# Layer 0's gated layer: the down projection with the output turned, 512 tokens moving, and the combine weights multiplied into the hidden values

## The chip, the core and the metric

The kernel runs on one core of a Trainium2 chip. The metric is the device time of one execution in microseconds (us), a median of several runs. The engines go by the profile's names: PE is TensorE's matmul and PEld its weight load, DVE is VectorE, ACT is ScalarE, POOL is GpSimd, SP is SyncE, which here only issues DMAs. Every engine works through its own instructions in order and waits on semaphores for the others. PE's clock is granted at one of two levels, 1.2 or 2.4 GHz; the profile writes it as a share of the higher one.

## The reference

Four layers run one after the other on 1,024 tokens (2 batches of 512) of 256 values, each with an attention-like step and a feed-forward step, all with a residual. The change lies in the feed-forward step of layer 0: a gated layer with 8 experts of 1,024 hidden values, all of which see all tokens; every expert's output is scaled by a combine weight of the token.

```python
router_probs = softmax(einsum('bsh,he->bse', x, w_router))
gate_weights = softmax(einsum('bsh,he->bse', x, w_gating) / 0.1)
g = einsum('bsh,ehf->ebsf', x, w_gate)
u = einsum('bsh,ehf->ebsf', x, w_up)
h = silu(g) * u
expert_out = einsum('ebsf,efh->ebsh', h, w_down)
cw = router_probs * gate_weights
cw = cw / (sum(cw, axis=-1, keepdims=True) + 1e-09)
out = einsum('ebsh,bse->bsh', expert_out, cw)
```

`x` here is the layer-normalised input. Since the combine weight of a token and an expert is one number, it may be multiplied into the expert's output or into `h`.

## The kernel before

`gated_layer_phase` (L1039) handles the layer as 32 units of 256 hidden values, four to an expert. Every float32 operand of a matmul is split into a high and a low part, and each product is made of three matmuls (`mm3`, L70: L73 high by high, L74, L75). A unit has four quarters q (L1113): two halves of 128 hidden values by two halves of 512 tokens.

For each unit:

- SP loads the gate and up weights (L1089, 512 KB) and the down weights (L1092, 256 KB), two units ahead at most.
- ACT makes the high parts of the gate and up weights (L1149, a unit ahead), POOL the low parts (L1189); the same for the down weights (L1177, L1202).
- PE computes gate and up of a quarter (L1121 to L1125): 12 matmuls, weights stationary, 512 tokens moving, into one of two gate banks and one of two up banks of PSUM.
- ACT takes silu of the gate (L1157), DVE multiplies it with up (L1217) into `hidden`, which has two slots; ACT rounds that to `h_hi` (L1162) and DVE subtracts to `h_lo` (L1223).
- PE computes the down projection (L1132 to L1139): for 8 chunks of 128 tokens, `h` is stationary and the 256 columns of the down weights move; 6 matmuls to a chunk, 48 to a unit, two chunks to a bank, 12 matmuls after each of which `out_done` counts.
- DVE adds each chunk, times the token's combine weight, to the residual `x` (L1241): 8 instructions to a unit.

The order of the work is written out by hand: `periods` (L1075) gives each engine the periods 0 to 32, the middle 30 of them as a hardware loop of two periods. In period n, PE does gate and up of unit n and then the down projection of unit n - 1, so that the elementwise chain of a unit has the next unit's gate and up (and the one before's down projection) to run beside. Period 32 has only the last down projection. The order on ACT in a period is silu 0, silu 1, high 0, the next unit's gate and up split, silu 2, high 1, silu 3, high 2, high 3, down split.

The router (`l0_router`, L978) runs between periods 0 and 1 (`route(eng)`, L1078): PE makes the logits with 48 matmuls of 16 columns (L1006), DVE and ACT the two softmaxes and the weights `g.cw`, tokens on partitions (L1011 to L1030). Its first user is L1241 in period 1. Ahead of period 0 stands the layer norm (`normaliser`, L159): PE turns the normalised tokens, ACT and DVE write them as `xnT_hi` and `xnT_lo` (L191), in two halves of tokens; PE's first gate matmul needs only the first half (L1116). After the last period DVE also takes the next norm's statistics (L139) of each two chunks as they are done.

Layer 1's expert phase (`l1_experts_phase`, L1426), which the change leaves as it is, already has the form that the change gives to layer 0: its weights are turned on PE (L1377), copied by ACT (L1387), stored by SP to `cw_rows` in DRAM (L1521), loaded back as rows spread over partitions (L1508, two loads of 256 KB for a unit), multiplied in by DVE (L1681), its down projection has stationary weights and 512 tokens moving, adds up in four PSUM banks over all units, and is at the end copied by ACT (L1635), turned back on PE (L1582) and added to `x` by DVE (L1691).

Of the kernel before, what the change touches and what calls it, by code (L numbers as in the profile page):

```python
# [977 lines left out]
def l0_router(nc, ctx, g, d, logits, logits_read):  # L978
# [10 lines left out]
    loaded, split_done = g.sem("r0_loaded"), g.sem("r0_split_done")  # L989
    logits_done, shifted_done, exp_done = g.sem("logits0_done"), g.sem("shifted0_done"), g.sem("exp_r0_done")  # L990
    dve_steps = g.sem("r0_dve_steps")

    def on_sync(sp):
        sp.dma_start(w_raw[:, :, :], d["wr0"]).then_inc(loaded, 16)

    def on_gpsimd(pool):
        split_on_pool(pool, w_raw, w_hi, w_lo, loaded, split_done)

    def on_scalar(act):
        act.wait_ge(shifted_done, 1)  # L1000
        act.activation(exps[:, :, 0, :], shifted[:, :, 0, :], ACT.Exp).then_inc(exp_done, 1)
        act.activation(exps[:, :, 1, :], shifted[:, :, 1, :], ACT.Exp, scale=10.0).then_inc(exp_done, 1)

    def on_tensor(pe):
        pe.wait_ge(split_done, 2)
        router_logits(pe, logits, N, (g.xnT_hi, g.xnT_lo), (w_hi, w_lo)).then_inc(logits_done, 1)  # L1006

    def on_vector(dve):
        own = Chain(dve, dve_steps)
        dve.wait_ge(logits_done, 1)  # L1010
# [4 lines left out]
        dve.sem_inc(shifted_done, 1)  # L1015
        dve.sem_inc(logits_read, 4)
        dve.wait_ge(exp_done, 2)
# [14 lines left out]
        own.wait()  # L1032

    r = Shared()
    r.on_sync, r.on_gpsimd, r.on_scalar, r.on_tensor, r.on_vector = on_sync, on_gpsimd, on_scalar, on_tensor, on_vector
# [3 lines left out]
def gated_layer_phase(nc, g, d, tag, N, weights, make_router):  # L1039
# [6 lines left out]
    with ExitStack() as ctx:  # L1046
# [9 lines left out]
        silu, hidden = sb("silu", [P, 2, 512]), sb("hidden", [P, 2, 512])  # L1056
        gate = ctx.enter_context(nc.psum_tensor(f"gate_{tag}", [P, 2, 512], F32))
        up = ctx.enter_context(nc.psum_tensor(f"up_{tag}", [P, 2, 512], F32))
        out = ctx.enter_context(nc.psum_tensor(f"out_{tag}", [P, TC // 2, 2, D], F32))

        def sem(name):
            return g.sem(f"{name}_{tag}")

        gu_loaded, dn_loaded = [sem("gu_loaded0"), sem("gu_loaded1")], [sem("dn_loaded0"), sem("dn_loaded1")]
        gu_hi_done, gu_lo_done, dn_hi_done, dn_lo_done = sem("gu_hi_done"), sem("gu_lo_done"), sem("dn_hi_done"), sem("dn_lo_done")
        gu_done, silu_done, hidden_done = sem("gu_done"), sem("silu_done"), sem("hidden_done")
        h_hi_done, h_lo_done = sem("h_hi_done"), sem("h_lo_done")
        out_done = sem("out_done")
        out_free = sem("out_free")


        norm = normaliser(nc, ctx, g, tag, out[:, :, :, :].rearrange("p (h k) j e -> p h k (j e)", h=2))
        router = make_router(nc, ctx, g, d, out[:, 0, :, :].rearrange("p j e -> p (j e)")[:, 0:TC * 16].rearrange("p (c n) -> p c n", c=TC), out_free)

        def periods(eng, period, route):  # L1075

            period(0, 0, 1, 1)
            route(eng)  # L1078
            with eng.Fori(0, (N - 2) // 2) as i:
                period(2 * i + 1, 1, i + 1, i + 2)  # L1080
                period(2 * i + 2, 0, i + 2, i + 2)
            period(N - 1, 1, N // 2, None)
            period(N, 0, None, None)

        with nc.Block() as block:
            @block.sync
            def _(sp):
# [3 lines left out]
                def load_dn(n, s):  # L1091
                    sp.dma_start(dn_raw[s][:, :, :], weights[n, :, 2, :, :]).then_inc(dn_loaded[s], 16)  # L1092
# [5 lines left out]
                load_dn(1, 1)  # L1098
                with sp.Fori(0, (N - 2) // 2) as i:
                    for s in range(2):  # L1100
                        sp.wait_ge(gu_lo_done, 2 * i + s + 1)
                        load_gu(2 * i + s + 2, s)
                        sp.wait_ge(dn_lo_done, 2 * i + s + 1)
                        load_dn(2 * i + s + 2, s)

            @block.tensor
            def _(pe):
                def period(n, s, uses, next_uses):
                    first, has_gu = isinstance(n, int) and n == 0, uses is not None
                    if has_gu:  # L1110
                        pe.wait_ge(gu_hi_done, n + 1)
                        pe.wait_ge(gu_lo_done, n + 1)
                        for q in range(Q):  # L1113
# [12 lines left out]
                    if not first:  # L1126
# [3 lines left out]
                        pe.wait_ge(h_hi_done, Q * n)  # L1130
                        pe.wait_ge(h_lo_done, Q * n)
                        for b in range(TC // 2):  # L1132
                            pe.wait_ge(out_free, 4 * (n - 1) + b + 1)
                            for j in range(2):
                                t = slice((2 * b + j) * P, (2 * b + j + 1) * P)
                                for fc in range(FC):
                                    last = mm3(pe, out[:, b, j, :], (h_hi[o][:, fc, t], h_lo[o][:, fc, t]),
                                               (dn_hi[o][:, fc, :], dn_lo[o][:, fc, :]), j == 0 and fc == 0, fc == FC - 1)
                            last.then_inc(out_done, 1)  # L1139

                norm.on_tensor(pe)
                pe.sem_inc(out_done, 4)
                periods(pe, period, router.on_tensor)

            @block.scalar
            def _(act):
                def split_gu(n, s, uses):
# [3 lines left out]
                def period(n, s, uses, next_uses):  # L1151
# [7 lines left out]
                    def high(q):  # L1159
                        fc, half = divmod(q, 2)  # L1160
                        act.wait_ge(hidden_done, Q * n + q + 1)
                        act.activation(h_hi[s][:, fc, half * 512:(half + 1) * 512], hidden[:, q % 2, :], ACT.Copy).then_inc(h_hi_done, 1)  # L1162
# [3 lines left out]
                    if not (isinstance(n, int) and n == 0):  # L1166
                        act.wait_ge(out_done, 4 * n)
# [8 lines left out]
                    act.wait_ge(dn_loaded[s], 16 * uses)  # L1176
                    act.activation(dn_hi[s][:, :, :], dn_raw[s][:, :, :], ACT.Copy).then_inc(dn_hi_done, 1)  # L1177
# [5 lines left out]
                periods(act, period, router.on_scalar)  # L1183

# [23 lines left out]
            def _(dve):  # L1208
                def period(n, s, uses, next_uses):
                    first = isinstance(n, int) and n == 0  # L1210

                    def product(q):
                        dve.wait_ge(silu_done, Q * n + q + 1)
                        if not (first and q < 2):
                            dve.wait_ge(h_hi_done, Q * n + q - 1)
                            dve.wait_ge(h_lo_done, Q * n + q - 1)
                        dve.tensor_tensor(hidden[:, q % 2, :], silu[:, q % 2, :], up[:, q % 2, :], ALU.mult).then_inc(hidden_done, 1)  # L1217

                    def low(q):
                        fc, half = divmod(q, 2)  # L1220
                        t = slice(half * 512, (half + 1) * 512)
                        dve.wait_ge(h_hi_done, Q * n + q + 1)
                        dve.tensor_tensor(h_lo[s][:, fc, t], hidden[:, q % 2, :], f32(h_hi[s][:, fc, t]), ALU.subtract).then_inc(h_lo_done, 1)  # L1223

                    if uses is not None:
                        product(0)
                        product(1)
                        low(0)
                        product(2)
                        low(1)  # L1230
                        product(3)
                        low(2)
                        low(3)
                    if not first:
                        dve.wait_ge(out_free, 4 * n)
                        for b in range(TC // 2):
                            dve.wait_ge(out_done, 4 * n + b + 1)
                            for j in range(2):
                                c = 2 * b + j
                                weight = g.cw[:, c, bass.ds(n - 1, 1)]  # L1240
                                last = dve.scalar_tensor_tensor(g.x[:, c, :], out[:, b, j, :], weight, g.x[:, c, :], ALU.mult, ALU.add)  # L1241
                            last.then_inc(out_free, 1)
                            if uses is None:
                                dve.wait_ge(out_free, 4 * n + b + 1)
# [1775 lines left out]
```

## Time and profile before

| what | us |
|---|---|
| runs: 1546.78, 1550.95, 1555.5; median | 1550.95 |
| the profiled execution, its own time | 1558.52 |
| span of its instructions | 1556.7 |
| granted clock of PE, mean over the span | 0.943 of 2.4 GHz |
| PE busy | 1410.2 (91%) |
| DVE busy | 899.8 (58%) |
| ACT busy | 695.5 (45%) |
| POOL busy | 332.9 (21%) |
| DMA, bytes moved | 110.83 MB, 71 GB/s |

Busy time counts an engine's computing instructions only. Matmuls overlap: a row of 400 ns for one matmul does not mean that the next one starts 400 ns later, so the pace of PE is read from the starts, not from the lengths. A stretch view gives, for a stretch of the span, the busy time and number of instructions of each engine and the mean granted clock. A timeline row gives the start from the beginning of the span, the length, engine, line, output and inputs, and in brackets the idle time before it and who ended it. A line of a helper (L73 to L75, L191, L206, L139) stands for all who call it; the tile's name tells them apart.

### The profile page before, as it was taken

To read this page: it belongs to the slowest core of one execution; us is meant where nothing else is said; L and a number is where in the kernel's file an instruction comes from. 1 tells how busy PE (TensorE), PEld (TensorE's weight loads), DVE (VectorE), ACT (ScalarE), POOL (GpSimd) and SP (SyncE) were. 2 spreads that over 40 slices of the span, in tenths; PEclk is the share of its full clock that TensorE was granted. 3 is DMA by queue.
4 is the path that set the end of the run, shared out by engine and by line. 5 is a ranking of instruction groups with operands and counts; after the bars stand their busy time and mean duration, and the time that the engine had idled before them with its cause. 6 is when DMAs were issued, how large, how long until landed. Compare 5 with 4: busy or idle time off the path is not lost. (4 is left out here: it accounts for less than half of the span.)

```text
span 1556.7 us, 24649 instructions
## 1 busy us (share of the span) xinstructions
PE 1410.2 (91%) x8362; PEld 1131.1 (73%) x8362; DVE 899.8 (58%) x1719; ACT 695.5 (45%) x1134; POOL 332.9 (21%) x348
## 2 busy tenths in 40 slices
PE   5799999799999999999998799999899786876994
PEld 4544444588888888888887777888678675765883
DVE  6778887655555555555556544444466455535556
ACT  5266667244344344344343265555443324443432
POOL 2101224212222222222221123333300033231100
PEclk8889999899999999999999799999999789897997
DMA  6811311111111111111100124555232115223000
GB/s 227 243 30 35 76 39 25 60 42 40 61 40 40 60 41 40 61 40 40 61 27 14 49 75 122 141 142 141 86 98 68 50 56 178 83 83 105 1 1 27
DMA packets 63703, 110.83 MB, mean 71 GB/s; under 512 B 10235, under 2 KB 39421, under 8 KB 62749
## 3 DMA queue, kind: packets, MB, share of 16 engines
q1 hardware_dynamic: 61773, 104.93, 23.1%
q0 software_dynamic: 1872, 5.13, 0.9%
q8 instruction: 36, 0.59, 0.2%
q14 instruction: 22, 0.18, 0.0%
HBM read 90.91 MB, written 18.97 MB: 71 GB/s over the span
## 5 line engine op out<-in xcount | busy, mean ns | idle before, releaser
L1217 DVE TENSOR_TENSOR hidden_l<-silu_l,up_l 128x512 f32<-128x512 f32 x128 | 88.1, 688 | 220.2 <-ACT silu_l L1157 220.2
L1157 ACT ACTIVATE silu_l<-gate_l 128x512 f32<-128x512 f32 x128 | 76.6, 599 | 308.6 <-PE up_l L75 308.6
L851 DVE TENSOR_REDUCE maxima<-a_scores 128x1 f32<-128x512 f32 x256 | 164.7, 685 | 41.0 <-PE a_scores L790 39.7
L73 PE MATMUL out_l<-dn_hi_l,h_hi_l 128*128 128x256 f32 x560 | 159.5, 285 | 5.4 <-DVE h_lo_l L2328 5.4
L818 ACT ACTIVATE probs<-b_scores 128x1024 f32<-128x1024 f32 x128 | 131.1, 1024 | 66.5 <-PE b_scores L747 64.5
L74 PE MATMUL out_l<-dn_lo_l,h_hi_l 128*128 128x256 f32 x560 | 159.1, 284 | 0.0
L75 PE MATMUL out_l<-dn_hi_l,h_lo_l 128*128 128x256 f32 x560 | 159.1, 284 | 0.0
L1189 POOL TENSOR_TENSOR gu_lo_l<-gu_raw_l,gu_hi_l 128x1024 fp32r<-128x1024 f32 x31 | 74.4, 2399 | 299.0 <-ACT gu_hi_l L1149 299.0
L73 PE MATMUL gate_l<-xnT_hi_n,gu_hi_l 128*128 128x512 f32 x280 | 112.6, 402 | 15.0 <-issue 11.8
L1241 DVE SCALAR_TENSOR_TENSOR x_sb<-out_l,cw,x_sb 128x256 f32<-128x256 f32 x256 | 109.0, 478 | 22.4 <-PE out_l L75 18.1
L73 PEld LDWEIGHTS out_l<-dn_hi_l,h_hi_l 128*128 128x128 f32 x560 | 108.4, 194 | 8.5 <-issue 5.9
L74 PE MATMUL gate_l<-xnT_lo_n,gu_hi_l 128*128 128x512 f32 x280 | 111.9, 400 | 0.0
L73 PE MATMUL up_l<-xnT_hi_n,gu_hi_l 128*128 128x512 f32 x280 | 111.7, 399 | 0.0
L75 PE MATMUL gate_l<-xnT_hi_n,gu_lo_l 128*128 128x512 f32 x280 | 111.5, 398 | 0.0
L74 PE MATMUL up_l<-xnT_lo_n,gu_hi_l 128*128 128x512 f32 x280 | 111.4, 398 | 0.0
L75 PE MATMUL up_l<-xnT_hi_n,gu_lo_l 128*128 128x512 f32 x280 | 111.2, 397 | 0.0
L74 PEld LDWEIGHTS out_l<-dn_lo_l,h_hi_l 128*128 128x128 f32 x560 | 108.2, 193 | 1.7
L75 PEld LDWEIGHTS out_l<-dn_hi_l,h_lo_l 128*128 128x128 f32 x560 | 108.0, 193 | 0.0
L1223 DVE TENSOR_TENSOR h_lo_l<-hidden_l,h_hi_l 128x512 fp32r<-128x512 f32 x128 | 102.3, 800 | 3.2
L1681 DVE TENSOR_TENSOR hidden_l<-silu_l,spread_l 128x512 f32<-128x512 f32 x64 | 44.3, 693 | 91.6 <-ACT silu_l L1608 91.6
L1608 ACT ACTIVATE silu_l<-front_l,b_l 128x512 f32<-128x512 f32 x80 | 55.0, 688 | 89.4 <-PE front_l L75 89.4
L790 PE MATMUL a_scores<-k_stack,q_stack 96*128 96x512 bf16 x256 | 85.1, 405 | 8.4 <-DMA q_stack<-q_stacks 5.4
(474 smaller groups left out, 3422.5 us busy)
## 6 DMA issues: line engine op xcount, KB each, us to landing
gu_raw_l<-w_units SPq DMA_DIRECT2D x32, 512.0 KB, 3.6
spread_l<-cw_rows SPq DMA_DIRECT2D x64, 256.0 KB, 3.9
dn_raw_l<-w_units SPq DMA_DIRECT2D x32, 256.0 KB, 2.7
k_stack<-k_stacks SPq DMA_DIRECT2D x8, 768.0 KB, 5.8
staged_l<-w_experts SPq DMA_DIRECT2D x24, 256.0 KB, 3.4
up_raw_l<-w SPq DMA_DIRECT2D x40, 128.5 KB, 3.5
dn_raw_l<-w SPq DMA_DIRECT2D x40, 128.0 KB, 2.1
phi_a<-fside SPq DMA_DIRECT2D x8, 512.0 KB, 3.3
```

The costliest lines, as they stand in the source:

```text
L73: pe.matmul(out, lhs[0], rhs[0], start=start, stop=False, skip_group_check=True)
L74: pe.matmul(out, lhs[0], rhs[1], start=False, stop=False, skip_group_check=True)
L75: return pe.matmul(out, lhs[1], rhs[0], start=False, stop=stop, skip_group_check=True)
L790: pe.matmul(a_scores[:, k % 2, :], q_stack[buf][0:MAXROW, h, at:at + P], k_stack[buf][0:MAXROW, h, kh * 512:(kh + 1) * 512], start=True, s ...
L818: act.activation(probs[u % 4][:, :, :], b_scores[:, u % 2, :, :], ACT.Exp, scale=SCALE).then_inc(exp_done, 1)
L851: dve.tensor_reduce(maxima[k // 16][:, i // 2, i % 2:i % 2 + 1], a_scores[:, k % 2, :], X, ALU.max).then_inc(a_read, 1)
L1157: act.activation(silu[:, q % 2, :], gate[:, q % 2, :], ACT.Silu).then_inc(silu_done, 1)
L1189: pool.tensor_tensor(gu_lo[s][:, :, :, :], gu_raw[s][:, :, :, :], f32(gu_hi[s][:, :, :, :]), ALU.subtract).then_inc(gu_lo_done, 1)
L1217: dve.tensor_tensor(hidden[:, q % 2, :], silu[:, q % 2, :], up[:, q % 2, :], ALU.mult).then_inc(hidden_done, 1)
L1223: dve.tensor_tensor(h_lo[s][:, fc, t], hidden[:, q % 2, :], f32(h_hi[s][:, fc, t]), ALU.subtract).then_inc(h_lo_done, 1)
L1241: last = dve.scalar_tensor_tensor(g.x[:, c, :], out[:, b, j, :], weight, g.x[:, c, :], ALU.mult, ALU.add)
L1608: act.activation(silu[:, q, :], up[:, q, :], ACT.Silu, bias=b1[s][:, :]).then_inc(silu_done, 1)
```

## The change

- **Down projection.** The down weights are stationary (128 hidden by 128 output values), 512 tokens of `h` move. A unit has 24 matmuls of 512 columns in place of 48 of 256. The sums stay in four PSUM banks (two halves of tokens by two halves of the outputs, turned) over all 32 units; only the first unit's down projection starts the banks.
- **Combine weights.** DVE multiplies `hidden` by `spread`, the unit's weights as a row on all 128 partitions, before `h_hi` and `h_lo` are made. `hidden` has four slots now. L1241 goes.
- **Router.** It runs ahead of period 0, on all engines, with its logits in the second gate bank, so PE waits for both halves of the norm first. After quarter 1 of unit 0, PE turns the weights into output banks (8 transposes), ACT copies them (after the split of unit 1's gate and up weights), SP stores them to DRAM, waits, and then loads the rows of units 0 and 1, spread. In the loop, SP loads unit n + 2's row once unit n's scaled values are done. Row and down weights share a semaphore.
- **Period 0.** ACT and DVE have another order in it: first all four silus and products, then the four scaled values, the four high and four low parts.
- **End.** ACT copies the four banks to `outT`, PE turns them back (16 transposes), and DVE adds them to `x` in four instructions with the statistics between them.
- Periods 1 and 2 are written out ahead of the loop (now 14 rounds of two periods).

The diff, cut to its core:

```diff
         def periods(eng, period, route):
+            route(eng)
             period(0, 0, 1, 1)
-            route(eng)
-            with eng.Fori(0, (N - 2) // 2) as i:
-                period(2 * i + 1, 1, i + 1, i + 2)
-                period(2 * i + 2, 0, i + 2, i + 2)
+            period(1, 1, 1, 2)
+            period(2, 0, 2, 2)
+            with eng.Fori(0, (N - 4) // 2) as i:
+                period(2 * i + 3, 1, i + 2, i + 3)
+                period(2 * i + 4, 0, i + 3, i + 3)
...
+                router.store_weights(sp)
+                load_spread(0, 0)
+                load_spread(1, 1)
                 with sp.Fori(0, (N - 2) // 2) as i:
                     for s in range(2):
                         sp.wait_ge(gu_lo_done, 2 * i + s + 1)
                         load_gu(2 * i + s + 2, s)
                         sp.wait_ge(dn_lo_done, 2 * i + s + 1)
                         load_dn(2 * i + s + 2, s)
+                        sp.wait_ge(hidden_done, Q * (2 * i + s + 1))
+                        load_spread(2 * i + s + 2, s)
...
                                 pe.wait_ge(silu_done, Q * n + q - 1)
-                                pe.wait_ge(hidden_done, Q * n + q - 1)
+                                pe.wait_ge(product_added, Q * n + q - 1)
+                            if first and q == 1:
+                                pe.wait_ge(router.shifted_done, 1)
+                            if first and q == 2:
+                                router.turn_weights(pe)
...
-                        for b in range(TC // 2):
-                            pe.wait_ge(out_free, 4 * (n - 1) + b + 1)
-                            for j in range(2):
-                                t = slice((2 * b + j) * P, (2 * b + j + 1) * P)
+                        for h in range(2):
+                            t = slice(h * 512, (h + 1) * 512)
+                            for dc in range(KC):
+                                e = slice(dc * P, (dc + 1) * P)
                                 for fc in range(FC):
-                                    last = mm3(pe, out[:, b, j, :], (h_hi[o][:, fc, t], h_lo[o][:, fc, t]),
-                                               (dn_hi[o][:, fc, :], dn_lo[o][:, fc, :]), j == 0 and fc == 0, fc == FC - 1)
+                                    last = mm3(pe, out[:, h, dc, :], (dn_hi[o][:, fc, e], dn_lo[o][:, fc, e]),
+                                               (h_hi[o][:, fc, t], h_lo[o][:, fc, t]), isinstance(n, int) and n == 1 and fc == 0, not has_gu and fc == FC - 1)
...
                     silu_of(0)
                     silu_of(1)
-                    if not (isinstance(n, int) and n == 0):
-                        act.wait_ge(out_done, 4 * n)
+                    if isinstance(n, int) and n == 0:
+                        split_gu(1, 1, 1)
+                        router.copy_weights(act)
+                        silu_of(2)
+                        silu_of(3)
+                        for q in range(Q):
+                            high(q)
+                        split_dn(s, uses)
+                        return
+                    act.wait_ge(down_returned, n)
                     high(0)
...
+                    def scale(q):
+                        half = q % 2
+                        if q == 0:
+                            dve.wait_ge(dn_spread_loaded[s], 32 * uses)
+                        dve.wait_ge(product_added, Q * n + q + 1)
+                        dve.tensor_tensor(hidden[:, q, :], hidden[:, q, :], spread[s][:, half * 512:(half + 1) * 512], ALU.mult).then_inc(hidden_done, 1)
...
+                    if first:
+                        for q in range(Q):
+                            product(q)
+                        for q in range(Q):
+                            scale(q)
+                        for q in range(Q):
+                            low(q)
+                        return
+                    dve.wait_ge(h_lo_done, Q * n)
+                    product(0)
+                    scale(0)
+                    product(1)
+                    scale(1)
+                    low(0)
...
+                for m in range(TC // 2):
+                    dve.wait_ge(down_returned, N + 2 * KC + m + 1)
+                    dve.tensor_tensor(g.x[:, 2 * m:2 * m + 2, :], g.x[:, 2 * m:2 * m + 2, :],
+                                      back[m].rearrange("p (j e) -> p j e", j=2), ALU.add).then_inc(product_added, 1)
+                    dve.wait_ge(product_added, Q * N + m + 1)
+                    take_stats(dve, g, (2 * m, 2 * m + 1))
```

## Rows read from the trace of the kernel before

**Rows 1.** Stretch view, 14 units: length, each engine's busy us, clock, DMA share, GB/s.

```profile
586.21:819.45 233.24, 233.24 (x1345) 206.73 (x1344) 126.34 (x224) 93.81 (x147) 51.77 (x28) 1.00 0.14 45
```

**Rows 2.** Groups by line of 28 units (busy us, mean ns | idle before, releaser).

```profile
L1241 DVE SCALAR_TENSOR_TENSOR x_sb<-out_l,cw,x_sb 128x256 f32<-128x256 f32 x224 | 95.4, 478 | 19.7 <-PE out_l L75 15.8
L1223 DVE TENSOR_TENSOR h_lo_l<-hidden_l,h_hi_l 128x512 fp32r<-128x512 f32 x112 | 89.6, 800 | 2.8
L1217 DVE TENSOR_TENSOR hidden_l<-silu_l,up_l 128x512 f32<-128x512 f32 x112 | 77.1, 688 | 191.3 <-ACT silu_l L1157 191.3
L1157 ACT ACTIVATE silu_l<-gate_l 128x512 f32<-128x512 f32 x112 | 67.1, 599 | 272.1 <-PE up_l L75 272.1
L1149 ACT ACTIVATE gu_hi_l<-gu_raw_l 128x1024 fp32r<-128x1024 f32 x28 | 29.5, 1054 | 0.0
```

**Rows 3.** Time order on PE, one unit: first matmul of down, gate/up, down (start, length).

```profile
586.21 0.28 PE L73 MATMUL out_l<-dn_hi_l,h_hi_l 128*128 128x256 f32 x1
591.97 0.40 PE L73 MATMUL gate_l<-xnT_hi_n,gu_hi_l 128*128 128x512 f32 x1
602.87 0.28 PE L73 MATMUL out_l<-dn_hi_l,h_hi_l 128*128 128x256 f32 x1
```

**Rows 4.** Time order on PE, layer 1's experts: a down projection's first matmul, and the next.

```profile
1004.58 0.40 PE L73 MATMUL out_l<-h_hi_l,dn_hi_l 128*128 128x512 f32 x1
1007.35 0.40 PE L73 MATMUL front_l<-xnT_hi_n,up_hi_l 128*128 128x512 f32 x1
```

**Rows 5.** Time order at the layer's front: normaliser, router logits, router, first down projection.

```profile
302.77 2.47 DVE L191 TENSOR_TENSOR xnT_lo_n<-out_l,xnT_hi_n 128x512 fp32r<-128x512 f32 x4
...
321.90 0.36 PE L75 MATMUL out_l<-wr_hi_r,xnT_lo_n 128*128 128x16 f32 x1
322.54 0.36 PE L75 MATMUL out_l<-wr_hi_r,xnT_lo_n 128*128 128x16 f32 x1
322.94 0.29 DVE L1011 TENSOR_REDUCE top<-out_l 128x16 f32<-128x128 f32 x1 [3.19 <-PE out_l L75]
326.23 0.68 DVE L1030 TENSOR_TENSOR cw<-both,total 128x64 f32<-128x64 f32 x4
...
336.31 0.28 PE L73 MATMUL out_l<-dn_hi_l,h_hi_l 128*128 128x256 f32 x1
```

**Rows 6.** The stretch view: first gate matmuls; after the logits; PE idle since 294.65.

```profile
305.30:307.70 2.40, 2.40 (x7) 1.86 (x6) 0.00 (x0) 0.31 (x1) 0.00 (x0) 0.50 0.26 106
...
322.70:328.00 5.30, 5.30 (x13) 4.16 (x14) 3.14 (x15) 1.68 (x3) 0.00 (x0) 0.50 0.35 137
...
297.00:298.00 1.00, 0.00 (x0) 0.00 (x0) 0.64 (x8) 0.90 (x1) 0.00 (x0) 0.76 0.00 0
```

**Rows 7.** Time order in layer 1: its weights turned, copied, stored, spread.

```profile
919.54 1.03 PE L1377 MATMUL front_l<-ident_sb,exps 128*64 128x128 f32 x8
...
920.61 1.02 ACT L1387 ACTIVATE cwT<-front_l 64x1024 f32<-64x1024 f32 x1 [1.61 <-PE front_l L1377]
...
921.66 0.55 SPq L1521 DMA_DIRECT2D cw_rows<-cwT  x1
924.66 1.17 SPq L1508 DMA_DIRECT2D spread_l<-cw_rows  x2
```

**Rows 8.** DMA issues (KB, median us to landing); landing of layer 1's 64 spread loads.

```profile
gu_raw_l<-w_units SPq DMA_DIRECT2D x32, 512.0 KB, 3.6
...
DMA to landing us min/median/max: 3.4/3.9/4.9
```

**Rows 9.** Time order at the end: gated layer's last matmul and statistics; layer 1's.

```profile
847.50 0.28 PE L75 MATMUL out_l<-dn_hi_l,h_lo_l 128*128 128x256 f32 x1
...
849.18 0.75 DVE L139 BATCH_NORM_STATS2 stats_sb<-x_sb 128x6 f32<-128x256 f32 x2
...
1116.66 0.39 PE L75 MATMUL out_l<-h_hi_l,dn_lo_l 128*128 128x512 f32 x1
...
1122.37 0.75 DVE L139 BATCH_NORM_STATS2 stats_sb<-x_sb 128x6 f32<-128x256 f32 x2
```

More of the change, by code:

```diff
@@ L975, in router_logits, with l0_router @@
     return last
-def l0_router(nc, ctx, g, d, logits, logits_read):
+def l0_router(nc, ctx, g, d, logits, banks):
     def sb(name, shape, dt=F32):
@@ L1066, in gated_layer_phase @@
         gu_done, silu_done, hidden_done = sem("gu_done"), sem("silu_done"), sem("hidden_done")
[L1067 to L1073, printed above, removed]
+        h_outT_done, h_lo_done = sem("h_hi_or_outT_done"), sem("h_lo_done")
@@ new lines, in period, with with_halves, return_output @@
+                        if has_gu:
+                            last.then_inc(down_returned, 1)
+                def with_halves(pe):
+                    norm.wait_half(pe, 0)
+                    norm.wait_half(pe, 1)
+                    router.on_tensor(pe)
+                def return_output(pe):
+                    for h in range(2):
+                        pe.wait_ge(h_outT_done, Q * N + KC * (h + 1))
+                        for c in range(4):
+                            for dc in range(KC):
+                                last = pe.transpose(back[2 * h + c // 2][:, c % 2 * D + dc * P:c % 2 * D + (dc + 1) * P],
+                                                    outT[:, h, dc, c * P:(c + 1) * P], g.ident[:, :])
+                            if c % 2 == 1:
+                                last.then_inc(down_returned, 1)
@@ L1147, in split_gu, with copy_output @@
+                def copy_output(act):
+                    for h in range(2):
+                        for dc in range(KC):
+                            act.wait_ge(down_returned, N + KC * h + dc + 1)
+                            act.activation(outT[:, h, dc, :], out[:, h, dc, :], ACT.Copy).then_inc(h_outT_done, 1)
                 def split_gu(n, s, uses):
@@ L1175, in period @@
                     high(3)
[L1176 to L1177 removed]
+                    split_dn(s, uses)
                 norm.root(act)
@@ L1221, in low @@
                         t = slice(half * 512, (half + 1) * 512)
[L1222 to L1244, printed above, removed]
-                                take_stats(dve, g, (2 * b, 2 * b + 1))
+                        dve.wait_ge(h_outT_done, Q * n + q + 1)
+                        dve.tensor_tensor(h_lo[s][:, fc, t], hidden[:, q, :], f32(h_hi[s][:, fc, t]), ALU.subtract).then_inc(h_lo_done, 1)
+                    if uses is None:
+                        return
[6 more added lines that the diff above has]
+                            low(q)
+                        return
+                    dve.wait_ge(h_lo_done, Q * n)
[4 more added lines that the diff above has]
+                    low(0)
+                    product(2)
+                    scale(2)
+                    low(1)
+                    product(3)
+                    scale(3)
+                    low(2)
+                    low(3)
                 norm.moments(dve)
```

79 lines of the change are left out of this document (54 added, 25 removed).

## The prediction

> **What bounds the kernel now.** The page shows PE busy for 91% of the span, but busy time hides the pace of matmuls, so I read the layer that changes stage by stage. The stretch view of 14 of its units [rows 1] has PE busy for all of 233.24 us at the full clock: 16.66 us a unit. DVE is busy 126 us of it, ACT 94, POOL 52, the DMA engines 0.14. No PE wait is left in the steady part, so only PE work taken out shortens it. The time order on PE [rows 3] splits a unit: 48 matmuls of the down projection, 256 columns each, from 586.21 to 591.97, 5.76 us or 0.120 each; 48 of gate and up, 512 columns each, to 602.87, 10.90 us or 0.227 each. The columns are the same (48 x 256 = 24 x 512), but two narrow matmuls take 0.240 and a wide one 0.227. That difference is what the change can win; what it moves to the front and the end of the layer is what it pays.
>
> **Steady part: minus 9.9 us.** A unit's down projection becomes 24 wide matmuls. At the pace of gate and up, which have the same form and stand between the same engines' work, they take 24 x 0.227 = 5.45 us, 0.31 less [rows 3]. Layer 1's down projection is nearer in operands (stationary down weights, banks kept over units) and slower: 12 in 2.77 us, 0.231 each [rows 4], so 5.54 us and 0.22 less. I take the first, since the surroundings are this layer's own, and keep the second as the end: 32 units give 9.9, at worst 7.0 us. No row shows wide matmuls faster than 0.227 over a unit, so I allow no more gain.
>
> The Trainium skill speaks against this: "TensorE: Matmul & The Clock Gate", section "Wait — 56ns, not 53.3ns?", states a fixed cost of about 2.5 ns for each warm matmul above its columns. By it, an estimate, 24 matmuls fewer would give 0.06 us a unit and 1.9 us in all. The trace disagrees: 0.120 us is 13 ns above 256 columns at 2.4 GHz, and 0.227 is 14 above 512 [rows 3].
>
> DVE loses 8 instructions of L1241 at 478 ns, 3.8 us a unit, and gains 4 multiplications, 2.8 us at the 688 ns of L1217 [rows 2]. Both lie beside PE and are worth nothing. The new chain of a unit (product, scale, high, low) is one multiplication a quarter longer. After the last quarter's silu come product and scale 3 at 0.69 each, low 2 and low 3 at 0.80 and ACT's work between them, some 4 us in all; PE needs them only after a down projection (5.45) and the next gate and up (10.9). Only the last unit has just the 5.45 us as cover, and there POOL's down split comes after it with about half a us to spare by my count. SP's new loads, 512 KB a unit, bring the DMA share of 0.14 [rows 1] to less than 0.3. SP waits for the scaled values before a row is loaded, and the next gate load is queued behind that; it is needed a period and a half later. The loop written out further changes no work.
>
> **Front: plus 11.7 us.** Before, the first down projection starts at 336.31 [rows 5]. I build its start after the change.
> - PE waits for both halves of the norm, which DVE ends at 302.77 + 2.47 = 305.2 [rows 5]. The clock then is at 0.50, the 1.2 GHz level [rows 6], after an idle PE. The 48 logit matmuls run there: three take from 321.90 to 322.54 at that level, 0.213 each [rows 5], so 10.2 us, to 315.6. That the clock is still low behind the logits, I take from the place behind them before the change, where it stood at 0.50 for 5.3 us with 13 gate matmuls [rows 6].
> - So the first 13 gate and up matmuls of unit 0 take 5.3 us again, the other 35 take 35 x 0.227 = 7.9, the 8 transposes 1.0 [rows 7]: unit 0 ends at 329.8. Unit 1's first two quarters, 5.45 us, end at 335.3.
> - Beside this runs the way of the weights. DVE's router needs 326.23 + 0.68 - 322.94 = 4.0 us from the logits [rows 5] and is done at 320, ahead of PE, so it costs nothing. PE turns the weights after quarter 1, at 315.6 + 5.3 + 11 x 0.227 = 323.4. ACT then has silu 1 (to 324.2), the split of L1149 (1.05, to 325.3; [rows 2]) and the copy (1.02, to 326.3; [rows 7]). From store to spread load layer 1 takes 924.66 - 921.66 = 3.0 [rows 7]: 329.4. The 512 KB row lands after 3.6 us by the gate load of the same size, 3.9 by the median of layer 1's half as large rows, 4.9 by their slowest [rows 8]; two of those one after the other, 9.8, are my far end. I take 4.2, a little above both medians: 333.6.
> - Only then can DVE scale: 4 x 0.69, 4 low parts at 0.80, and the product 0 of unit 1 at 0.69 [rows 2], 6.65 us, all in DVE's order, to 340.2. ACT's high parts, its down split and silu 0 of unit 1 are queued in the same way and end earlier. PE's quarter 2 of unit 1 needs the bank that this product frees. So **PE stands from 335.3 to 340.2**, 4.9 us; SP's gate load for unit 2 waits behind the store too, but has until about 342.
> - After a PE idle since 294.65 the clock's mean was already 0.76 in the stretch 297 to 298 [rows 6], so I expect it to fall in this gap as well. What it costs is 5.3 us for 13 matmuls that take 2.95 at full pace, 2.35. The two remaining quarters then take 5.45 + 2.35, and the first down projection starts at 348.0, **11.7 us later**. If the clock holds, 9.4.
>
> **End: plus 4.0 us.** Before, DVE follows the last down projection bank by bank, and the statistics end 849.18 + 0.75 - 847.50 = 2.4 us after PE's last matmul starts. Layer 1's end has the new form, copies, transposes, then four additions with statistics that DVE does one after the other: 1122.37 + 0.75 - 1116.66 = 6.5 us [rows 9]. The row is the same form and the same shapes, so I give it no more than half a us either way.
>
> **Sum.** 11.7 + 4.0 - 9.9 = +5.8 us. The profiled execution's own time of 1558.52 would become 1564.3. It is 7.6 us above the median of the runs shown; the terms are differences, so they hold for either, and on the median of 1550.95 the sum gives **1556.8 us**, 0.4% slower. A difference of 0.5%, 7.75 us, is about what a measurement of this kernel can tell from none, so my forecast is no change that can be told, on the slow side.
>
> **The rivals.**
> - *The row of weights lands late, and the kernel is slower.* Place: unit 0's scale on DVE, with PE standing in unit 1. Each us of landing after 4.2 is a us of the end, since nothing behind it has slack. For it: no row shows a spread load of 512 KB, and unit 1's row and unit 2's gate weights are issued right behind it. Against it: 512 KB of gate weights land in 3.6 [rows 8]. It decides from a landing of 4.2 + 1.95 = 6.15 us on, where the sum passes 7.75; at the far end of 9.8 it is +11.4, 1562.4 us. Chance 0.2.
> - *PE does not stand.* If the weights come as early as PE can use them, unit 1 ends at 329.8 + 10.9 = 340.7, the front costs 4.4, and the sum is 4.4 + 4.0 - 9.9 = -1.5: 1549.5 us. For it: ACT, DVE and SP may overlap more closely than row by row. Against it: the chain from 323.4 to 340.2 is in order throughout, with 4.9 us to make up. Chance 0.17.
> - *Wide matmuls gain less.* If a wide down matmul starts every 0.231 us as in layer 1 [rows 4], the gain is 7.0 and the sum +8.7, 1559.7 us. Chance 0.08. By the 2.5 ns of the Trainium skill's "TensorE: Matmul & The Clock Gate" (above), as an estimate, it would be 11.7 + 4.0 - 1.9 = +13.8, 1564.8 us.
> - *A real gain* needs front and end together below 2 us; I find no row for it, since the additions at the end alone cost 4.0.
>
> **How the numbers follow.** The forecast has 0.55. Its own range goes from 9.4 + 3.5 - 9.9 = +3.0 (the clock holds) to some +8. The range over all cases reaches down past the case without the stall, 1549.5, by the 2.5 us that a median of runs between 1546.78 and 1555.5 may well move, and up to the late row with the slower pace, 11.4 + 2.9 = +14.3: **1547 to 1565 us**. For the same reason I count part of each case on either side of the bound. Faster by over 0.5%: 0.06 (most from the case without the stall). Slower by over 0.5%: 0.17 of the forecast, 0.16 of the late row and 0.05 of the slower pace, 0.38. Within 0.5%: the rest, 0.56.
>
> **What would show it.** In the profile after the change: 24 wide down matmuls to a unit in about 5.45 us and a unit in 16.35, with PE never idle between; logits from about 305 to 316 at a granted clock of 0.5; a single PE gap of about 5 us before quarter 2 of unit 1, ended by DVE's product behind the spread load, and 1.2 GHz after it; the first down projection 12 us later than before; statistics 6.5 us after the last down matmul. The forecast is wrong if the unit does not get shorter, if PE waits in the steady part for the scaled values or the row, or if there is no gap in unit 1.

## The result and the profile after

The changed kernel takes 1557.93 us (median of 20 runs, 1550.62 to 1563.69), the kernel before 1553.17 (20 runs beside them, 1546.78 to 1557.01). The medians lie 4.8 us apart; over the runs the kernel takes 1.0034 times as long, 95% interval 1.0020 to 1.0048, which is 3.1 to 7.5 us more. The forecast was 5.8 us more, within half a per cent. It came out, but not by its own sum: two terms, the front and the steady part, were off in the same direction, by 3.4 us together, and part of the loss lies where the prediction did not look. That the total fits is in part luck.

One profiled execution gives the parts. The first rows are the stretch view of the kernel after (length; busy us of PE, PEld, DVE, ACT, POOL; clock; DMA share; GB/s): 14 units of the steady part, then the logits, the first gate matmuls, and the stretch behind PE's stand.

```profile
589.86:818.34 228.48, 228.48 (x1009) 189.19 (x1008) 121.94 (x169) 84.76 (x140) 56.70 (x28) 1.00 0.23 78
...
305.28:315.30 10.02, 10.02 (x48) 10.02 (x48) 0.00 (x0) 0.00 (x0) 0.00 (x0) 0.50 0.00 0
315.51:320.78 5.27, 5.27 (x14) 4.11 (x14) 3.14 (x15) 1.69 (x3) 0.00 (x0) 0.50 0.00 0
...
337.99:341.40 3.41, 3.41 (x8) 2.73 (x9) 2.69 (x4) 1.58 (x2) 1.04 (x2) 0.52 0.44 165
```

A unit takes 228.48 / 14 = 16.32 us instead of 16.66 [rows 1], with PE busy throughout. The logits run at 0.50, 10 us long, and the gate matmuls behind them at 0.50 for 5.27 (5.30 before [rows 6]).

The time order of the kernel after shows one unit (first matmuls of down, gate, next down), then the layer's front and its end (start, length, what ended the wait before it).

```profile
589.86 0.39 PE L73 MATMUL out_l<-h_hi_l,dn_hi_l 128*128 128x512 f32 x1
...
595.30 0.39 PE L73 MATMUL gate_l<-xnT_hi_n,gu_hi_l 128*128 128x512 f32 x1
...
606.18 0.39 PE L73 MATMUL out_l<-h_hi_l,dn_hi_l 128*128 128x512 f32 x1
...
305.28 0.35 PE L73 MATMUL gate_l<-wr_hi_r,xnT_hi_n 128*128 128x16 f32 x1 [2.70 <-DVE xnT_lo_n L191]
...
323.54 1.03 PE L1039 MATMUL out_l<-ident_sb,cw 128*32 128x128 f32 x8
...
326.20 0.34 SPq L1048 DMA_DIRECT2D cw_rows<-cw0T  x1
328.20 0.33 SPq L1124 DMA_DIRECT2D spread_l<-cw_rows  x1
332.21 2.50 DVE L1297 TENSOR_TENSOR hidden_l<-hidden_l,spread_l 128x512 f32<-128x512 f32 x4 [0.80 <-DMA spread_l<-cw_rows]
334.63 2.49 DVE L1303 TENSOR_TENSOR h_lo_l<-hidden_l,h_hi_l 128x512 fp32r<-128x512 f32 x4
337.15 0.69 DVE L1290 TENSOR_TENSOR hidden_l<-silu_l,up_l 128x512 f32<-128x512 f32 x1
337.99 0.77 PE L73 MATMUL gate_l<-xnT_hi_n,gu_hi_l 128*128 128x512 f32 x1 [2.49 <-DVE hidden_l L1290]
...
345.06 0.39 PE L73 MATMUL out_l<-h_hi_l,dn_hi_l 128*128 128x512 f32 x1
...
845.32 0.40 PE L75 MATMUL out_l<-h_hi_l,dn_lo_l 128*128 128x512 f32 x1
...
846.19 0.69 DVE L1340 TENSOR_TENSOR x_sb<-x_sb,gate_l 128x512 f32<-128x512 f32 x1 [7.89 <-PE gate_l L1193]
...
851.04 0.75 DVE L139 BATCH_NORM_STATS2 stats_sb<-x_sb 128x6 f32<-128x256 f32 x2
```

Down takes 5.44 us where [rows 3] had 5.76. In the front, read the releasers: DVE was idle for only 0.80 us until the row of weights landed, then worked in order for 5.6 us, and PE stood 2.49 us for the product at its end. The first down projection starts at 345.06 against 336.31 [rows 5], and the statistics end 6.47 us behind the start of the last down matmul, against 2.4 [rows 9].

All kernels of this study were read in these parts. Front: from the layer's first aggregate on DVE (296.53 after, 297.14 before) to the first down matmul. Middle: to the start of the last one. End: to the end of the last statistics. Layer 1: from its own first aggregate to that of the next phase. Single runs of one kernel differ by up to 13 us, and the longer ones were granted the lower mean clock (kernel after: 1550.62 us at 0.943, 1563.69 at 0.932); the parts of layer 0 and layer 1 repeat within 0.15 us (last two rows of the table against the first two). Each ratio is to runs of the kernel before that were made beside that kernel (medians of 1551.91 to 1553.80 us).

| kernel | front | middle | end | layer 0 | layer 1 | median us (runs) | ratio to before, 95% |
|---|---|---|---|---|---|---|---|
| before | 39.17 | 511.19 | 2.43 | 552.79 | 252.88 | 1553.17 (20) | |
| after | 48.53 | 500.26 | 6.47 | 555.26 | 254.07 | 1557.93 (20) | 1.0034 (1.0020 to 1.0048) |
| e1_narrow | 48.27 | 511.19 | 6.36 | 565.82 | 249.20 | 1567.86 (6) | 1.0095 (1.0072 to 1.0118) |
| e2_row_ready | 46.08 | 500.25 | 6.47 | 552.80 | 250.83 | 1555.84 (1) | |
| e3_order | 46.20 | 500.36 | 6.46 | 553.02 | 250.72 | 1553.30 (12) | 1.0000 (0.9984 to 1.0016) |
| e4_before_router_first | 43.38 | 511.19 | 2.42 | 556.99 | 250.74 | 1554.71 (1) | |
| e5_front | 37.21 | 504.04 | 6.47 | 547.72 | 251.05 | 1549.84 (12) | 0.9970 (0.9956 to 0.9983) |
| e6_end | 48.43 | 501.16 | 4.62 | 554.21 | 252.18 | 1554.98 (1) | |
| e7_both | 37.22 | 504.91 | 4.63 | 546.76 | 251.00 | 1549.55 (12) | 0.9975 (0.9960 to 0.9991) |
| e8_early_gate | 37.18 | 501.28 | 4.63 | 543.09 | 254.10 | 1544.65 (6) | 0.9948 (0.9934 to 0.9962) |
| e9_after_again | 48.45 | 500.25 | 6.47 | 555.17 | 254.06 | 1558.88 (1) | |
| e10_before_again | 39.18 | 511.19 | 2.42 | 552.79 | 252.89 | 1554.88 (1) | |

### The profile page after: what moved, and what is told of

The parts are those of the page before. It is cut to its first block and busy times, and to the rows that moved or that the text cites. A ratio compares the mean times of both kernels' runs of the same rounds, so it can differ in the third digit from the quotient of the medians.

```text
span 1556.3 us, 22704 instructions
## 1 busy us (share of the span) xinstructions
PE 1407.6 (90%) x7618; PEld 1099.0 (71%) x7618; DVE 888.1 (57%) x1595; ACT 679.4 (44%) x1124; POOL 343.8 (22%) x348
## 5 line engine op out<-in xcount | busy, mean ns | idle before, releaser
L73 PE MATMUL out_l<-h_hi_l,dn_hi_l 128*128 128x512 f32 x416 | 162.2, 390 | 0.8 <-POOL dn_lo_l L1749 0.8
L75 PE MATMUL out_l<-h_hi_l,dn_lo_l 128*128 128x512 f32 x416 | 162.6, 391 | 0.0
L74 PE MATMUL out_l<-h_lo_l,dn_hi_l 128*128 128x512 f32 x416 | 162.5, 391 | 0.0
L1265 POOL TENSOR_TENSOR gu_lo_l<-gu_raw_l,gu_hi_l 128x1024 fp32r<-128x1024 f32 x31 | 84.8, 2735 | 270.2 <-ACT gu_hi_l L1217 270.2
L1297 DVE TENSOR_TENSOR hidden_l<-hidden_l,spread_l 128x512 f32<-128x512 f32 x128 | 108.4, 849 | 7.2 <-DMA spread_l<-cw_rows 0.8
L1230 ACT ACTIVATE h_hi_l<-hidden_l 128x512 fp32r<-128x512 f32 x128 | 80.0, 626 | 34.1 <-DVE hidden_l L1297 34.1
L73 PEld LDWEIGHTS out_l<-h_hi_l,dn_hi_l 128*128 128x128 f32 x416 | 78.3, 188 | 18.4 <-issue 1.2
L74 PEld LDWEIGHTS out_l<-h_lo_l,dn_hi_l 128*128 128x128 f32 x416 | 78.2, 188 | 17.1
L75 PEld LDWEIGHTS out_l<-h_hi_l,dn_lo_l 128*128 128x128 f32 x416 | 78.1, 188 | 16.6
```

The source lines that it names most:

```text
L73: pe.matmul(out, lhs[0], rhs[0], start=start, stop=False, skip_group_check=True)
L74: pe.matmul(out, lhs[0], rhs[1], start=False, stop=False, skip_group_check=True)
L75: return pe.matmul(out, lhs[1], rhs[0], start=False, stop=stop, skip_group_check=True)
L1265: pool.tensor_tensor(gu_lo[s][:, :, :, :], gu_raw[s][:, :, :, :], f32(gu_hi[s][:, :, :, :]), ALU.subtract).then_inc(gu_lo_done, 1)
L1297: dve.tensor_tensor(hidden[:, q, :], hidden[:, q, :], spread[s][:, half * 512:(half + 1) * 512], ALU.mult).then_inc(hidden_done, 1)
```

## The experiments

**e1_narrow: what makes the unit shorter.** In the down projection:

```
+ for part in range(2):                      # 256 tokens each
+     t = slice(h * 512 + part * 256, ...)
-     mm3(pe, out[:, h, dc, :], (dn...), (h_hi[o][:, fc, t], ...))
+     mm3(pe, out[:, h, dc, a], (dn...), (h_hi[o][:, fc, t], ...))
```

> The kernel after with one thing undone: the down projection moves 256 tokens in one matmul, 48 matmuls of 256 columns to a unit instead of 24 of 512; operands, banks, order and everything else stay. Theory (a matmul costs some 14 ns above its columns here, so two narrow ones take 0.240 us and a wide one 0.227): first to last down matmul goes from 500.3 us to the 511.2 us of the kernel before, 0.34 us a unit; the layer and the time grow by 10.9 us, to about 1569. Rival (the fixed cost of a matmul is 2.5 ns, as the Trainium skill's page TensorE: Matmul & The Clock Gate states, and the unit became shorter for another reason, the orientation or DVE's additions): 500.3 plus 1.9, 502.2 us, and about 1560.

Measured: the middle is 511.19 us, that of the kernel before to the hundredth, and 10.93 more than in the kernel after. Orientation, banks kept over the units and the work taken from DVE do nothing for it; the number of matmuls does everything. The theory holds, and the rival's 502.2 is excluded. Every matmul here has a weight load of its own, so no run parts the cost of a matmul from that of its weight load.

**e2_row_ready: is it the way through DRAM that makes PE stand?**

```
+ spread[s] <- weights[s, 0:1, 0:2]   (s = 0, 1, ahead of store_weights)
  router.store_weights(sp)
- load_spread(0, 0); load_spread(1, 1)
```

> The kernel after, but the rows of weights of units 0 and 1 are filled from the gate weights in DRAM, right behind the first loads, so that no row waits for router, turn, copy and store (units 0 and 1 are therefore scaled by other numbers; the store still runs, behind the two loads). Theory A, the prediction's (the way of the weights through DRAM makes PE stand in unit 1): the gap of 2.5 us and the low clock behind it go, and the first down projection starts 3.9 us earlier, 44.6 us after the layer's first aggregate instead of 48.5. Theory B (DVE was idle for only 0.8 us before the first scale; its order, four scales and four low parts ahead of unit 1's product 0, makes PE stand): the gap shrinks by 0.8, to 1.7 us, still ended by product 0, and the first down projection comes about 1 us earlier.

Measured, from the time order and the stretch view of e2_row_ready:

```profile
337.54 0.69 DVE L1291 TENSOR_TENSOR hidden_l<-silu_l,up_l 128x512 f32<-128x512 f32 x1
338.37 0.47 PE L73 MATMUL gate_l<-xnT_hi_n,gu_hi_l 128*128 128x512 f32 x1 [1.60 <-DVE hidden_l L1291]
```

```profile
338.37:341.77 3.40, 3.40 (x15) 2.85 (x16) 2.70 (x4) 1.98 (x3) 1.03 (x2) 1.00 0.54 181
```

PE still stands, for 1.60 instead of 2.49 us: theory B. But the clock stays at 1.00 behind the shorter stand, and so the front shrinks by 2.45 us and not by 1: 0.9 of standing and the 1.6 that the low clock had cost.

**e3_order: DVE's order.** Two more buffers of hidden; DVE and ACT of unit 0:

```
  for q in range(Q): product(q)
+ product(0, 1); product(1, 1)        # unit 1's
  for q in range(Q): scale(q)
```

> The kernel after with another order in the first two units: DVE makes unit 1's products 0 and 1 (in two further buffers of hidden) ahead of unit 0's scales, and ACT makes the two silus ahead of unit 0's high parts; the way of the weights is as it was. Theory B (DVE's order sets the gap): no gap in unit 1, the clock stays up, unit 1 ends 2.5 + 1.4 us earlier and the first down projection starts 44.6 us after the layer's first aggregate (48.5 before this edit); the time falls by 3.9, to about 1554. Theory A (the landing sets it): PE stands in front of the first down projection instead, for as long as it stood before, and the first down stays near 48. Rival C (the stall is only moved on): the first down is earlier, but unit 1's own scales are now late, a gap of 1 to 2 us appears before the second down projection, and the layer gains less than 2 us.

None of the three. The stand in unit 1 is gone, as B says; the front gains 2.3 us and not 3.9, since PE now stands in front of the first down projection, but not for the row, as A had it. Time order of e3_order:

```profile
339.67 0.62 ACT L1207 ACTIVATE dn_hi_l<-dn_raw_l 128x512 fp32r<-128x512 f32 x1
340.44 2.19 POOL L1281 TENSOR_TENSOR dn_lo_l<-dn_raw_l,dn_hi_l 128x512 fp32r<-128x512 f32 x1 [12.47 <-ACT dn_hi_l L1207]
...
342.73 0.47 PE L73 MATMUL out_l<-h_hi_l,dn_hi_l 128*128 128x512 f32 x1 [1.96 <-POOL dn_lo_l L1281]
```

The down weights had long been loaded, but ACT splits them behind four high parts, and GpSimd's low part follows. That queue had been hidden under the stand. GpSimd's low part also took 2.19 us here, beside DVE's low parts, and 1.30 with DVE idle beside it (kernel after, 348.64); the last section says more of this pair. The middle stays at 500.36, so rival C, a stand that is only moved on, is out too. The runs fall by more than layer 0's 2.24 us, because layer 1 is 3.35 shorter as well (below).

**e4_before_router_first: the move alone.**

```
- period(0, 0, 1, 1); route(eng)
+ route(eng); period(0, 0, 1, 1)      # PE: both halves of the norm first
```

> The kernel before with the router alone moved ahead of unit 0, behind both halves of the norm, as in the kernel after; additions on DVE, narrow down projection and everything else as before. Theory (the logits at the low clock cost 10.2 us where they took 5.9 behind unit 0; the start 1.1 us later because both halves are waited for; only one low stretch with gate matmuls instead of one and a half, minus 1.7): the first down projection starts 3.7 us later than in the kernel before, 42.9 us after the layer's first aggregate instead of 39.2. Rival (48 logit matmuls cost the same wherever they stand): at most 1.5 us later, 40.7.

Measured: 4.21 us (43.38 against 39.17), half a us above the theory's 3.7 and far from the rival's 1.5. Its stretches are those of the kernel after: logits 10.24 us and the gate matmuls behind them 5.26, all at 0.50. The move of the router is thus nearly half of the front's 9.36; the turn (0.8), the stand (2.49) and the low clock behind it (1.6) make 4.9 of the other 5.15.

**e5_front: another order of the front.** On e3_order:

```
+ unit 0 on PE: q0, logits of chunks 0-3, q1, logits 4-7, q2, q3
+ unit 1: turn_weights, q0 ... q3; down(0): wait for h=0, then for h=1
+ ACT: split_dn(0) ahead of the high parts; split_gu(2) between them
+ DVE, unit 0: scales and low parts of h=0, then of h=1; router between products 1 and 2
- route(eng)
```

> The kernel after with the front put in another order (steady part and end as they are): gate and up of unit 0 start behind the first half of the norm; the logits stand in a bank of the down sums, 24 of them behind quarter 0 and 24 behind quarter 1; the weights are turned ahead of unit 1; unit 1's products 0 and 1 come ahead of unit 0's scales in two further buffers; the first down projection waits for each half of the tokens by itself. Theory (the front of the kernel after costs 9.4 us because logits and 13 gate matmuls run at the low clock, PE starts 1.1 us later, and PE stands for 2.5 us): 24 logits between wide matmuls leave the clock up, the low clock is paid once (some 8 gate matmuls), PE does not stand, and the first down projection starts 39 to 41 us after the layer's first aggregate (48.5 in the kernel after, 39.2 in the kernel before); the time falls by 8, to about 1550, 3 us under the kernel before. Rival A (logits bring the clock down wherever they stand): 42 to 44 us. Rival B (the row of weights lands too late for the earlier down projection): PE stands in front of the first down by 3 us or more, 42 to 44 us, at full clock until then.

Measured: the front is 37.21 us, 2 under the kernel before; ratio 0.997. Neither rival A nor B, and better than the theory, since here the first quarter of unit 0 ran at 1.00 as well (0.50 in the kernel before [rows 6]). Stretch view of e5_front, the first quarter, both groups of logits and the gate matmuls behind the second:

```profile
304.72:307.53 2.81, 2.81 (x12) 2.33 (x13) 1.05 (x2) 0.84 (x1) 0.00 (x0) 1.00 0.00 0
307.53:310.13 2.60, 2.60 (x26) 2.59 (x24) 0.69 (x1) 0.60 (x1) 0.00 (x0) 1.00 0.00 0
312.96:315.56 2.60, 2.60 (x26) 2.60 (x24) 0.69 (x1) 2.38 (x3) 0.42 (x1) 1.00 0.00 0
315.56:319.99 4.43, 4.43 (x15) 3.47 (x15) 3.14 (x15) 2.13 (x4) 1.95 (x1) 0.61 0.03 6
```

24 logits between wide matmuls run at full clock in 2.60 us, and the clock falls only behind the second group. The first quarter takes 2.81 us; in the time order of the kernel before it takes 4.49, from the first gate matmul of this quarter to that of the next:

```profile
304.19 0.77 PE L73 MATMUL gate_l<-xnT_hi_n,gu_hi_l 128*128 128x512 f32 x1 [1.01 <-DVE xnT_lo_n L191]
...
308.68 0.39 PE L73 MATMUL gate_l<-xnT_hi_n,gu_hi_l 128*128 128x512 f32 x1
```

That is 1.7 of the 2.0 us. It was not forecast: PE stands for 4.86 us ahead of the normaliser's transposes in both kernels, and why the clock was up again sooner in e5_front is not shown. Without it the front would take 38.9 us, about the lower end of the theory's 39 to 41. The middle lost 3.8 us again, by a stand inside the first down projection. Time order of e5_front:

```profile
334.41 3.49 DVE L1315 TENSOR_TENSOR hidden_l<-hidden_l,spread_l 128x512 f32<-128x512 f32 x2
334.59 2.76 POOL L1279 TENSOR_TENSOR gu_lo_l<-gu_raw_l,gu_hi_l 128x1024 fp32r<-128x1024 f32 x1 [1.26 <-ACT gu_hi_l L1217]
...
339.44 0.47 PE L73 MATMUL out_l<-h_hi_l,dn_hi_l 128*128 128x512 f32 x1 [1.80 <-DVE h_lo_l L1321]
```

Two scales take 3.49 us and end at 337.90, half a us after GpSimd's low part (337.35).

**e6_end: the end overlapped.** In the last period:

```
+ if (h, dc) == (1, KC - 1): return_output(pe, 0)   # ahead of the last bank
```

> The kernel after with the end overlapped: the sums of the first 512 tokens are turned back between the last two banks of the down projection instead of behind all of them, so that DVE's first two additions with their statistics run beside PE's last bank. Theory (the 6.5 us behind the last down matmul are DVE's four additions with statistics, 5.6 us, behind a copy and transposes): the last statistics end about 1.1 us earlier, 554.2 us for the layer instead of 555.3. Rival (copy and transposes of the second half set the end): less than 0.4 us.

Measured: layer 0 is 1.05 us shorter, 554.21, as the theory says. PE's last down matmul starts 0.9 later, behind the transposes, and DVE ends 1.05 earlier: DVE's four additions set the end, but for 0.32 us for which DVE now waits for the second half's transposes.

**e7_both** is e5_front with e6_end.

> The edits of e5_front and e6_end together, output complete. Theory: the two add, since one lies ahead of the first and the other behind the last down projection: 9 us less than the kernel after, about 1549, ratio to the kernel before 0.997. Rival (one of the two is given back in the other's place): no more than the better of the two alone.

Measured: layer 0 shrinks by 8.50 us; 7.54 and 1.05 alone. They add in the profile. The runs can't tell e7_both from e5_front: its ratio is 0.9975 (0.9960 to 0.9991), and the gain of 1 us is below what they resolve. They also show less than the profile does: to the end of layer 1 the profile is 7.95 us ahead of the kernel before, the runs 3.9 (1.4 to 6.2).

**e8_early_gate: GpSimd out of DVE's way.** On e7_both:

```
+ load_gu(2, 0)                  # SP, ahead of store_weights
+ split_gu(2, 0, 2)              # ACT, behind copy_weights
+ split_gu(2, 0)                 # GpSimd, in period 0
```

> e7_both with one more edit: unit 2's gate weights are loaded ahead of the store of the router's weights, and ACT and GpSimd split them before the row of weights lands instead of between unit 0's second scales. Theory (in e5_front DVE's second pair of scales, 334.41 to 337.90, took 3.49 us where two take 1.38, because GpSimd's low part of the gate weights ran from 334.59 to 337.35 and a DVE multiplication with both operands in SBUF cannot run beside it): the two scales take 1.4 us, PE no longer stands in front of the second half of the first down projection (1.8 us) and the clock does not fall behind it; first to last down shrinks by 3.8 us, from 504.9 to 501.1, and the time to about 1546, 0.995 of the kernel before. Rival (DVE waited for ACT or for the row, not for GpSimd): the scales stay at 3.5 us and nothing is gained.

Measured, time order of e8_early_gate:

```profile
334.03 1.28 DVE L1325 TENSOR_TENSOR hidden_l<-hidden_l,spread_l 128x512 f32<-128x512 f32 x2
```

The two scales take 1.28 us, the stand is gone, and the middle is 501.28 us (3.6 less). The theory holds, the rival is out. 1544.65 us, ratio 0.9948: the fastest kernel of the study, under the kernels before and after. The gain lies in layer 0, 9.70 us shorter than before; layer 1 is 1.2 us longer. The profiled execution, 1549.52 us, is the slowest of its six.

**e9_after_again, e10_before_again: where the rest of the loss lies.** No edit.

> The kernel after, unchanged, once more. Its profile showed layer 0 longer by 2.5 us, the runs the whole by 4.8; its layer 1 took 254.1 us against 252.9, with the clock at 0.50 for 10 us from the layer's aggregate where the kernel before had 5. Theory (the clock in layer 1's front differs from execution to execution): layer 0 again takes 555.3 us within 0.3, layer 1 another time than 254.1, by 1 us or more. Rival (layer 1 is longer because of the change): 254.1 within 0.5, and the clock again at 0.50 for 10 us.

> The kernel before, unchanged, once more, for the same question. Theory (from execution to execution): layer 0 again takes 552.8 us within 0.3, layer 1 another time than 252.9 by 1 us or more. Rival (a property of the kernel): 252.9 within 0.5.

The rival holds, both times: layer 1 takes 254.06 and 252.89 us, as in the first profiles. It belongs to the kernel. In the stretch from 5 to 10 us behind layer 1's first aggregate, first the kernel after:

```profile
878.83:883.83 5.00, 4.46 (x13) 3.22 (x12) 2.15 (x4) 3.43 (x6) 0.55 (x1) 0.50 0.38 143
```

and the kernel before:

```profile
877.03:882.03 5.00, 3.95 (x20) 2.99 (x19) 2.85 (x5) 3.68 (x7) 0.55 (x2) 0.92 0.34 127
```

PE's work is the same there; it runs at 0.50 in the one and mostly at full clock in the other.

## Why the prediction was right, and where it was not

- **Steady part, forecast 9.9 us gained: 10.93.** 32 down projections at 5.44 instead of 5.76 give 10.2; the rest is gate and up, 10.88 instead of 10.90, 30 times. The first end, this layer's own pace, was the right choice; e1_narrow shows that it is the number of matmuls. By the 2.5 ns of the Trainium skill ("TensorE: Matmul & The Clock Gate", "Wait — 56ns, not 53.3ns?") 1.9, as an estimate, had to come out; the trace disagrees. DVE's multiplications are hidden, as said.
- **Front, forecast 11.7 us lost: 9.36.** The logits (10.02 us to the start of the last, forecast 10.2 in all), the gate matmuls behind them at the low clock (5.27, forecast 5.3) and the place and the releaser of the stand are as forecast. The failed step is the size of "PE stands from 335.3 to 340.2": 2.49 us, not 4.9. Store to spread load took 2.0 us, not the 3.0 of [rows 7]; DVE's chain from landing to the end of the product 5.6, not 6.65: four scales took 2.50 where 4 x 0.69 was counted, since consecutive DVE instructions overlap, and four low parts 2.49 where 4 x 0.80 was counted (0.80 is the mean of the steady part [rows 2]; here each took 0.68). The landing, 4.0, was within 0.2. Low clock behind the stand: 8 matmuls and 1.6 us, not 13 and 2.35. That the row's way makes PE stand is only a third of it: e2_row_ready takes 0.9 of 2.49 away, and the other 1.60 is DVE's order, which e3_order removes from unit 1. Against these 3.1 us saved, PE came to the stand 0.8 us later than counted (335.50, which is 336.1 in the kernel before's time), most of it because the logits began 0.7 late; a smaller part is that the low stretch behind them holds 12 gate and up matmuls where 13 were counted.
- **End, forecast 4.0 us lost: 4.04.**
- **Sum, forecast +5.8: +2.47 in layer 0,** and +1.2 in layer 1, where the prediction has no term because no instruction changed. From the first aggregate to the end of layer 1 that is 3.6 us in one pair of profiles and 3.5 in the other. The runs' 4.8, with 3.1 to 7.5 as interval, holds this; behind layer 1 the spans of the profiles differ by up to 5 us (427.0 to 431.8) with no order by kernel that I see. So the number was better than its steps: the loss in layer 1, which it had not counted, made up for a part of what the front and the steady part were off.
- **The rivals.** The row landed in 4.0 us, so "late" is out; PE does stand; the wide matmuls gain 10.93, more than was forecast. A real gain needed front and end below 2 us: e8_early_gate has front and end at 0.2 us over the kernel before (37.18 + 4.63 against 39.17 + 2.43), and there it is.

## What to carry to other kernels

Merging narrow matmuls paid here what the trace's pace per matmul said, within 1 us of 10, and that is little; what such a change moves ahead of the loop and behind it cost more and is where to work. When a long wait goes, look at what is queued behind the same releaser on each engine: here GpSimd's low part of the down weights, and then DVE held up by GpSimd, were next. A row of small matmuls was better laid between wide ones: two groups of 24 took 2.60 us each in e5_front, 48 in one stretch 5.9 behind unit 0 (kernel before, from 316.84) and 10 at the layer's start (kernel after).

## What the hardware showed that was not expected

- **DVE and GpSimd block each other.** A scale (both operands in SBUF) takes 692 ns in the median and up to 2892 in e5_front, where it started beside GpSimd's low part; with that moved, e8_early_gate has two in 1.28 us. In the steady part of the kernel after the same pair meets once in every unit (scale up to 1385 ns, GpSimd's gate low part 2761 in the median and 2386 at best), hidden under PE. The Trainium skill ("SBUF — State Buffer", "SBUF: two separate sides") states it as an exclusive lock, held for the whole instruction, between a DVE instruction with two SBUF inputs and a GpSimd instruction that reads SBUF, as the low part does. The trace agrees: the scale ends at 337.90, 0.55 us behind the end of GpSimd's 2.76, which is less than one scale's length.
- **The length of PE's stand does not decide the clock alone.** After 2.49 us (kernel after) it was down to 0.50; after 1.60 (e2_row_ready) and 1.96 (e3_order) it stayed at 1.00; after 1.80 in e5_front it fell less than a us behind PE's restart and cost 11 matmuls 1.7 us. What tells these apart is open.
- **A change in layer 0 moved the clock in layer 1.** Its first rise comes about 10 us behind that layer's aggregate in the kernel after, e1_narrow, e7_both and e8_early_gate, and about 5 us in the others; the kernels before and after, the two that were profiled again, repeat it. This rise alone does not set layer 1's time: e1_narrow rises late and has the shortest layer 1, since a second low stretch, 12 to 24 us behind the aggregate, is missing there. The time goes with the mean clock of the layer's first 25 us: 0.80 in e1_narrow (249.20 us), 0.73 to 0.76 in e2 to e5 and e7 (250.7 to 251.1), 0.69 and 0.68 in e6_end and the kernel before (252.2 and 252.9), 0.59 in the kernel after and e8_early_gate (254.1). What decides it was not tried. Stretch views of these 25 us, in order the kernels after, before and e1_narrow:

```profile
873.83:898.83 25.00, 22.67 (x94) 19.77 (x95) 10.03 (x26) 9.66 (x21) 5.06 (x7) 0.59 0.24 74
...
872.03:897.03 25.00, 22.16 (x99) 18.82 (x100) 12.02 (x28) 11.02 (x23) 5.33 (x8) 0.68 0.26 75
...
886.22:911.22 25.00, 22.67 (x115) 19.49 (x116) 11.32 (x28) 14.36 (x27) 6.00 (x8) 0.80 0.29 85
```
